# Adding the experts' results to rows in memory with accumulating scatters, and copying those rows to the output, in an attention and mixture-of-experts block

## The reference

```python
xn  = layernorm(x)
# attention: 16 heads of 8, causal
q, k, v = split(xn @ w_qkv)
a   = softmax(mask(q @ k.T / sqrt(8))) @ v @ w_proj + b_proj + xn
a   = layernorm(a) * gamma + beta
# experts: softmax over 8, the two best kept with their probabilities
y   = 0
for e in range(8):
    y += combine[:, e] * (gelu(xn @ W1[e] + b1[e]) @ W2[e] + b2[e])
out = x + a + y
```

## Time and profile before

| | |
|---|---|
| median of three runs | 837.65 us |
| the profiled execution | 838.32 us |
| its span, first to last instruction | 836.6 us |
| PE busy | 698.7 us (84%) |
| DVE busy | 653.4 us (78%) |
| POOL busy | 557.4 us (67%) |
| ACT busy | 544.8 us (65%) |
| moved by DMA | 93.66 MB, mean 112 GB/s |

### The profile page before, as it was taken

How to read it: one execution, slowest core, us unless ns; L and a number is a source line. 1 busy time by engine, 2 the same in 40 slices (tenths; PEclk the granted TensorE clock), 3 DMA queues, 4 the chain that set the end, 5 groups by cost and what they waited for, 6 DMA issues and landing times.

```text
span 836.6 us, 25028 instructions
## 1 busy us (share of the span) xinstructions
PE 698.7 (84%) x7876; PEld 518.2 (62%) x7878; DVE 653.4 (78%) x1550; ACT 544.8 (65%) x1107; POOL 557.4 (67%) x611
## 2 busy tenths in 40 slices
PE   2766989999999999999988878659999999999800
PEld 1543556666666666666656555338988889888700
DVE  5877978888978787878888887637878888888644
ACT  4812646666666666666756656538989999999700
POOL 8521758888877777777887786616766677667700
PEclk9987989999999999999999999869999999999955
DMA  9691323232322232223243333102222222222189
GB/s 271 230 312 59 94 68 100 89 102 89 101 90 100 91 100 91 99 92 107 84 148 120 111 107 93 28 14 73 87 83 80 86 87 82 86 77 90 49 277 333
DMA packets 113313, 93.66 MB, mean 112 GB/s; under 512 B 16618, under 2 KB 97650, under 8 KB 113268
## 3 DMA queue, kind: packets, MB, share of 16 engines
q1 hardware_dynamic: 95508, 70.26, 26.9%
q0 software_dynamic: 8704, 18.17, 6.1%
q10 hardware_dynamic: 9056, 4.66, 1.9%
HBM read 43.85 MB, written 48.93 MB: 111 GB/s over the span
## 4 chain that ended last, share of the span: by engine, by line
PE 60%; DVE 11%; ACT 7%; issue 7%; DMA 6%; POOL 6%; SPq 2%; ACTq 0%; POOLq 0%; DVEq 0%
PE wide L1323 11%; PE bank_head L1212 9%; PE bank_head L1314 5%; PE bank_maxB L1314 5%; PE wide L1177 5%; PE bank_maxA L1191 5%; DVE shift L966 4%; DMA xn_rows<-parts_dram 3%; PE bank_maxB L1191 3%; PE bank_maxA L1195 3%; PE wide L1181 3%; PE bank_misc L1237 3%; DMA pieces_f<-in_w 3%; POOL probs L601 2%; PE bank_maxB L1195 2%
## 5 line engine op out<-in xcount | busy, mean ns | idle before, releaser
L653 POOL DMA_INDIRECT parts_dram<-o_T,dest x144 | 161.3, 1120 | 75.9 <-issue 48.5
L601 POOL TENSOR_SCALAR_AFFINE_SELECT probs<-probs 128x512 f32<-128x512 f32 (+1 forms) x192 | 152.3, 805 | 83.1 <-ACT probs L687 81.0
L687 ACT ACTIVATE probs<-wide 128x1024 f32<-128x1024 f32 x192 | 185.4, 1023 | 31.1 <-PE wide L1177 18.9
L966 DVE TENSOR_REDUCE shift<-bank_maxA 128x2 f32<-128x512 f32 (+1 forms) x192 | 132.3, 689 | 52.4 <-PE bank_maxA L1195 48.7
L592 POOL DMA_INDIRECT x_slots<-xn_rows,slot_i x128 | 131.3, 1026 | 38.9 <-issue 37.5
L966 DVE TENSOR_REDUCE shift<-bank_maxB 128x2 f32<-128x512 f32 (+1 forms) x192 | 131.6, 685 | 5.4 <-PE bank_maxB L1195 1.3
L731 ACT ACTIVATE probs<-wide,b_all 128x256 f32<-128x256 f32 x288 | 121.5, 478 | 16.6 <-PE wide L1323 10.9
L1212 PE MATMUL bank_head<-probs,v_aug 128*32 128x256 f32 (+1 forms) x2048 | 99.6, 336 | 27.5 <-DVE x L992 22.9
L1323 PE MATMUL wide<-xgT_raw,xnT 128*128 128x256 f16 x864 | 109.3, 277 | 6.5 <-DVE xgT_raw L1073 6.5
L1212 PEld LDWEIGHTS bank_head<-probs,v_aug 128*32 128x32 f32 x2048 | 60.3, 112 | 72.3 <-issue 35.0
L1056 DVE TENSOR_TENSOR probs<-probs 128x512 f16<-128x512 f32 x144 | 99.7, 693 | 5.5 <-ACT probs L737 1.1
(11 more groups left out here) (178 smaller groups left out, 1253.3 us busy)
## 6 DMA issues: line engine op xcount, KB each, us to landing
qk_rows<-split SPq DMA_DIRECT2D x32, 512.0 KB, 3.0
x_slots<-fill SPq DMA_DIRECT2D x16, 598.5 KB, 7.8
fill<-x_slots SPq DMA_DIRECT2D x72, 133.0 KB
q_diag<-qk_rows SPq DMA_DIRECT2D x256, 32.0 KB, 1.8
k_cat<-qk_rows SPq DMA_DIRECT2D x64, 128.0 KB, 2.1
xn_rows<-parts_dram SPq DMA_DIRECT2D x8, 1024.0 KB, 11.7
x_all<-in_x SPq DMA_DIRECT2D x8, 512.0 KB, 7.5
pieces_f<-in_w SPq DMA_DIRECT2D x8, 512.0 KB, 4.0
```

The costliest lines, as they stand in the source:

```text
L601: pool.affine_select(out=part, in_=part, compare_op=ALU.is_ge, fill=0.0, base=0, pattern=[[0, n], [1, P]], channel_multiplier=-1).then_inc ...
L653: pool.indirect_dma_start(out=parts_dram, out_offset=bass.IndirectOffsetOnAxis(ap=dest[:, of, t:t + 1].bitcast(U32), axis=0), in_=y[:, of ...
L687: act.activation(probs[:, u, :], ps[:, :], ACT.Exp, scale=SCALE).then_inc(empty, 1)
L966: V.tensor_reduce(dst, ps[:, :].rearrange("p (j k) -> p j k", j=nh), axis=AX.X, op=ALU.max, negate=True).then_inc(empty, 1)
```

## The change

The rows that will be the output are now in memory from the start of the experts. `sum_rows` holds one row per token and the spare rows. During attention, SP stores each sequence's part of `x_all`, once the attention's result has been added to it (`begin_out(b)`, 32 stores of 128 KB). POOL's indirect DMAs then add their rows to `sum_rows` in memory (`compute_op=ALU.add`). A token has two picks with different experts, and two additions to one row must not be under way at once: so where the expert changes between two tiles, POOL waits until the three tiles before have landed. Whether it changes is worked out in registers from the packed list of experts: `whole` is 32 then, else 0, and with 0 the wait asks for nothing that is not there already. At the end, SP and ACT copy `sum_rows` to the output in four transfers from memory to memory, with no part in on-chip memory. The numbers behind a row lose one, so that a row of `xn_rows` has 132 elements and not 133.

```diff
-        parts_dram = nc.dram_tensor("parts_dram", [2 * B * T + NS * S, D], F32).ap()
+        sum_rows = nc.dram_tensor("sum_rows", [B * T + NS * S, D], F32).ap()
...
+            def begin_out(b):
+                sp.wait_ge(res_ready, b + 2)
+                sp.nop(nofuse=True)
+                sp.dma_start(sum_rows[bass.ds(b * T, T), :].rearrange("(t p) d -> p t d", p=P),
+                             x_all[:, bass.ds(b * QT, QT), :]).then_inc(out_begun, 16)
+            def stores(s):
+                return s - 2 - LAST >= 0 if isinstance(s, int) else True
...
+                if stores(s):
+                    begin_out(s - 2 - LAST)
...
             for u in range(2):
-                sp.wait_ge(sent[u], 32 * (NT // 2))
+                sp.wait_ge(sent[u], 32 * (NT // 2 - DEST_BUFS // 4))
+            for u in range(DEST_BUFS):
+                sp.wait_ge(placed[u], FIRST)
...
                 sp.dma_start(xg[:, quad, :, :], x_slots[bass.ds(s * S, S), :].rearrange("(t p) d -> p t d", p=P)).then_inc(xg_loaded[quad], 16)
+                if isinstance(s, int) and s in (1, 2):
+                    begin_out(B - 3 + s)
...
-            both = parts_dram[0:2 * B * T, :].rearrange("(t p c) d -> p t (c d)", p=P, c=2)
-            for c in range(LAST_CHUNKS):
-                if c >= PART_BUFS:
-                    sp.wait_ge(out_ready, c - PART_BUFS + 1)
-                sp.dma_start(parts[:, c % PART_BUFS, :, :], both[:, LC * c:LC * (c + 1), :]).then_inc(parts_loaded[c % PART_BUFS], 16)
+                sp.wait_ge(placed[u], 32 * (NS // DEST_BUFS) + FIRST)
+            for c in range(0, OUT_CHUNKS, 2):
+                rows = B * T // OUT_CHUNKS
+                sp.dma_start(out.rearrange("b (t p) d -> (b t) (p d)", p=16)[rows // 16 * c:rows // 16 * (c + 1), :],
+                             sum_rows[rows * c:rows * (c + 1), :].rearrange("(t p) d -> t (p d)", p=16)).then_inc(out_stored, 16)
+            sp.wait_ge(out_stored, 16 * OUT_CHUNKS)
...
+            pool.wait_ge(out_begun, 16 * B)
+            EVEN = sum((E - 1) << BITS * j for j in range(0, FIELDS - 1, 2))
+            ODD = sum((E - 1) << BITS * j for j in range(1, FIELDS - 1, 2))
+            def changes_at(i):
+                experts = experts_of(pool, i)
+                steps_up = (experts >> BITS) - (experts & (EVEN + ODD))
+                return (steps_up & EVEN) + EVEN, (steps_up & ODD) + ODD
+            def tile(s, k, changes):
+                if hides(s):
+                    u = s - 1
+                    of = (k - 1) % DEST_BUFS
+                    if beyond(u, 0):
+                        whole = changes[k % 2] >> (BITS * (k + 1) - 5) & 32 if BITS * (k + 1) > 5 else changes[k % 2] << (5 - BITS * (k + 1)) & 32
+                        for back in range(1, Y_BUFS):
+                            if beyond(u, back - 1):
+                                before = (k - 1 - back) % DEST_BUFS
+                                rounds = (s - k) * 4 - (0 if k >= 1 + back else 32)
+                                pool.wait_ge(placed[before], whole + (rounds + FIRST))
+                    pool.wait_ge(y_ready, u * 2 + 2)
                     pool.nop(nofuse=True)
                     for t in range(2):
-                        pool.indirect_dma_start(out=parts_dram, out_offset=bass.IndirectOffsetOnAxis(ap=dest[:, of, t:t + 1].bitcast(U32), axis=0),
-                                                in_=y[:, of % Y_BUFS, t, :], in_offset=None).then_inc(placed[of], 16)
-            tiles(pool, tile, load=False)
+                        pool.indirect_dma_start(out=sum_rows, out_offset=bass.IndirectOffsetOnAxis(ap=dest[:, of, t:t + 1].bitcast(U32), axis=0),
+                                                in_=y[:, of % Y_BUFS, t, :], in_offset=None,
+                                                compute_op=ALU.add).then_inc(placed[of], 16)
...
-            for c in range(LAST_CHUNKS):
-                act.wait_ge(out_ready, c + 1)
-                act.dma_start(out.rearrange("b (t p) d -> p (b t) d", p=P)[:, LC * c:LC * (c + 1), :],
-                              x_all[:, LC * c:LC * (c + 1), :]).then_inc(out_stored, 16)
-            act.wait_ge(out_stored, 16 * LAST_CHUNKS)
+            for u in range(DEST_BUFS):
+                act.wait_ge(placed[u], 32 * (NS // DEST_BUFS) + FIRST)
+            for c in range(1, OUT_CHUNKS, 2):
+                rows = B * T // OUT_CHUNKS
+                act.dma_start(out.rearrange("b (t p) d -> (b t) (p d)", p=16)[rows // 16 * c:rows // 16 * (c + 1), :],
+                             sum_rows[rows * c:rows * (c + 1), :].rearrange("(t p) d -> t (p d)", p=16)).then_inc(out_stored, 16)
...
-                dve.wait_ge(parts_loaded[c % PART_BUFS], 16 * (c // PART_BUFS + 1))
-                V.tensor_tensor(mine[:, :, 0:D], mine[:, :, 0:D], mine[:, :, D:2 * D], ALU.add).then_inc(parts_added, 1)
-                dve.wait_ge(parts_added, c + 1)
-                V.tensor_tensor(here, here, mine[:, :, 0:D], ALU.add).then_inc(out_ready, 1)
```

More of the change, by code:

```diff
@@ L238, in attention_and_moe @@
         placed = [sem(f"placed{u}") for u in range(DEST_BUFS)]
-        parts_loaded = [sem(f"parts_loaded{u}") for u in range(PART_BUFS)]
-        parts_added = sem("parts_added")
-        out_ready = sem("out_ready")
+        out_begun = sem("out_begun")
+        spare_ready = sem("spare_ready")
         out_stored = sem("out_stored")
@@ L312, in beyond, with steps @@
             return s > n if isinstance(s, int) else True
-        def steps(eng, step, after=((), ()), first_tile=None, written_out=False):
+        assert STAGES % 2 == 1
+        def steps(eng, step, after=((), ()), first_tile=None, written_out=False, in_loop=STAGES - 1):
             experts = None
-            first_whole = STAGES - 1 if not written_out else TAIL
+            first_whole = in_loop if not written_out else TAIL
             count = TAIL - first_whole
@@ L488, in _ @@
             load_experts()
-            sp.wait_ge(consts, 29)
-            steps(sp, step)
+            sp.wait_ge(consts, 27)
+            steps(sp, step, in_loop=STAGES + 1)
             for u in range(2):
-                sp.wait_ge(sent[u], 32 * (NT // 2))
+                sp.wait_ge(sent[u], 32 * (NT // 2 - DEST_BUFS // 4))
+            for u in range(DEST_BUFS):
+                sp.wait_ge(placed[u], FIRST)
             sp.wait_ge(packing, EXPERTS_PACKED)
@@ L659, in _ @@
+            changes = changes_at(0)
+            for s in range(UNROLL):
+                tile(s, s, changes)
+            with pool.Fori(0, NS // UNROLL - 1) as i:
+                changes = changes_at(i + 1)
+                for k in range(UNROLL):
+                    tile(i * UNROLL + (UNROLL + k), k, changes)
+            tile(NS, 0, changes_at(NS // UNROLL))
         @block.scalar
@@ L753, in tile @@
                     before = (k - 2 - Y_BUFS) % DEST_BUFS
-                    later(act, placed[before], (s - k) * 4 + (32 if k >= 2 + Y_BUFS else 0), beyond(s, 1 + Y_BUFS))
+                    later(act, placed[before], (s - k) * 4 + (32 + FIRST if k >= 2 + Y_BUFS else FIRST), beyond(s, 1 + Y_BUFS))
                     act.wait_ge(xg_used, s * 2 - 2)
@@ L919, in weights @@
                 then(V.tensor_reduce(red[:, :], prob[:, :, :], axis=AX.X, op=ALU.add))
-                V.tensor_scalar(xn_rows[:, :, D + 4], best[:, 0, :], -1.0, float(E), ALU.mult, ALU.add).then_inc(route, 1)
+                V.tensor_scalar(xn_rows[:, :, D + 3], best[:, 0, :], -1.0, float(E), ALU.mult, ALU.add).then_inc(route, 1)
                 route_count += 1
```

55 lines of the change are left out of this document (22 added, 33 removed).

## The result

The changed kernel takes 891.11 us (median of 4 runs, 885.89 to 893.77) beside 836.44 for the kernel before (4 runs, 835.06 to 838.79): a ratio of 1.064 [1.061, 1.067]. The forecast was 820 with a range up to 866. The profiled execution took 893.8 us (span 892.1), 55.5 more than the 838.3 against which the sum was made.

A forecast was written before the change was run, and what follows sets the result against it. PE was taken to set the expert tiles' pace and DMA transfers the end. From 838.3 us, -24.0 (end), +5.0 (first tile) and +1 (last scatter) gave 820, range 811 to 866.

The forecast's parts named there:

- The accumulating scatters: POOL's 144 scatters in the expert stage: adding in memory costs 0 us more each (bounds 0 and 0.96); last landing +1.
- POOL becomes the bound: Rival: longer descriptor lists slow POOL's scatters; at 0.4 us more each 866 us, by the skill page 877; chance 0.29.
- The 32 stores: SP's stores of x_all during attention fit into its idle 1.05 us per step: cost 0, without that cover 14 us.
- The first tile: Start of the experts: tile 0's load waits behind four stores, the last needing sequence 29's addition: +5.0 us, bounds 0 and 8.
- The end: After the last scatter: a 4 MB copy within memory replaces loads, additions and stores: -24.0 us, bounds -26.6 and -11.6.
- a slow copy: Rival at the end: memory is read and written at once, the copy takes 27 us, total 833 us; chance 0.11.
- POOL's registers: POOL's extra register operations per tile, some 0.3 us, lie under 2.3 us of scatters: cost 0.
- additions don't overlap: Rival in the scatters: each addition waits for its own read, 8 us per tile, over 1100 us; chance 0.05.

The follow-up runs named there:

- e1: The changed kernel with plain scatters in place of accumulating ones, waits, stores and copy kept: 824.97 us, 0.987 of the kernel before.
- e3: The changed kernel adding only to spare rows, without waits at expert changes, each added row half as long (64 elements): 875.14 us, 1.048 of the kernel before.
- e5: The kernel before plus 32 stores of x_all that nothing reads, at the change's places in SP's queue: 846.76 us, 1.012.
- e6: The kernel before plus the same 32 unread stores, moved behind the q and k store and the first four tile loads: 834.54 us, 0.998.

## Why the prediction was wrong

**The step that failed is *The accumulating scatters*.** It took 0 us more per scatter, out of bounds of 0 and 0.96; the runs show 0.58 by the medians (1544 to 960 in e1) and 0.48 by the means (1602 to 1120). Its reason, that scatters of 133 and 128 elements cost the same, was sound for what it compares (e3: rows of half the length cost the same, too), but it says nothing about another form of the instruction. I had called the step the weakest and read from the trace that 0.08 us was all it could bear; with that known, a cost that no row bounded better than 0.96 deserved more of the chance than 0.29. The rest of the sum can be read from e1_plain, where a scatter does cost nothing more: 824.97 beside 820. By the four lines of the table above its profile differs from the kernel before by +5.0, +4.8, 0 and -23.0, against 0, +5.0, 0 and -23.0 in the sum: what is left over lies in the steps, where the stores are.

In the stage of 290.4 us, the scatters' 230.6 - 161.3 = 69.3 less the 23.6 that the prediction found free makes +45.7. Of the remaining 62.6 - 45.7 = 16.9 us, 16.2 are the seven changes of expert, where the prediction put 11 and let the free time pay for them. The seven gaps are 2.54 to 2.76 us long, of which 0.30 is there anyway, so each wait cost 2.2 to 2.5 us where the prediction had up to 1.6. The waits were thus sized too small by a third, and they lost their cover once POOL was the bound. With plain scatters (e1) they cost nothing, as predicted.

**The rival *POOL becomes the bound* came true**, beyond the 866 that its 0.4 us gave. Its price from the Trainium skill's page "Collectives: The Full Stack", section "The bandwidth ceiling: the fold count and why AG ≠ RS ≠ AR", was 0.48 us more and 877: the size that was then measured. But by its mechanism, a price for each row, 64 rows should have cost half as much more, 0.24, and they cost 0.53. A packet for each added row is in the trace; POOL's time hardly follows it. The agreement was one of size only, and luck.

The Trainium skill's other page, "DMA: Bandwidth & Descriptors", section "Anatomy of one DMA — SWDGE (gpsimd) path", says that writing descriptors is a small part that grows noticeably only with many of them; the trace agrees as far as rows stand for descriptors, 1.0 to 1.8 ns a row here. The prediction took it as a second reason, beside its rows, to call the addition free, and that doesn't follow: the measurement decides, 0.53 to 0.58 us for the form.

***The 32 stores*** were put at 0, with 14 us if their cover was gone; 9.4 us more stand at the end of the steps in the change's profile (the first line of the table). The idle 1.05 us that I read in the earlier trace rows is from the looped steps, and there the shift is small: SP's store of q and k stands at 378.04 before and at 380.55 in the change, after three quarters of the sequences, and 0.8 of these 2.5 us were there ahead of the first store of `x_all`. From then on the gap widens to 9.4. In those steps SP loads a piece of the weights right behind the shifts, ACT waits for it, and the store went ahead of it. That a queue has room in one step is no proof for the steps that carry something more. That the place is the cause is shown by e5 and e6. The 9.4 itself is too much for it: in the seven profiled kernels with the stores at these places the last store of q and k stands at 503.7 to 510.4 (median 506.1), in the five others at 497.8 to 501.9 (median 501.1), so the place costs some 5 us there and the rest is the difference of two executions.

***The first tile*** was right in its mechanism and near in size: +5.0 predicted, +5.9 in the table. The timelines of POOL, SP and PE show the addition of sequence 29 ending at 555.13, the four stores held up behind it, and a wait of 5.49 us.

```profile
554.41 0.72 POOL L624 TENSOR_TENSOR x_all<-x_all,y 128x256 f32<-128x256 f32 x1 [1.80 <-ACT y L769]
```

```profile
541.18 14.40 SPq L455 DMA_DIRECT2D sum_rows<-x_all  x4
556.00 0.89 SPq L521 DMA_DIRECT2D fill<-x_slots  x2
```

```profile
558.60 0.69 PE L1335 MATMUL bank_maxA<-ident,fill 128*128 128x128 f32 x2 [5.49 <-DMA fill<-x_slots]
```

***The end*** was right: -24.0 predicted for a copy of 14.6 us; it took 15.8 (876.28 to 892.1) where the end had taken 38.6, so -22.8; the last scatter's landing took 0.4 us longer where +1 was put. The rival of a slow copy fell. ***POOL's registers*** show no cost: where POOL is the bound, the gap between two scatters is 0.30, the least there was before. The rival that additions don't overlap fell too: a whole scatter has landed a median of 3.3 us after its start, where 8 us per tile had been feared.

With the measured terms put in their places the sum is 838.3 + 9.4 + 5.9 + 45.7 + 16.9 - 22.4 = 893.8; this only lays the two profiles end to end and proves nothing more. The gain at the end was real and as large as forecast; nearly three times as much was then lost on POOL.

## What to carry to other kernels

Before work is moved from one engine into the descriptors of another, count how many such instructions the receiving engine issues and how much time each may grow before that engine is the bound (here 0.08 us); if no row shows the new form, give the bound's upper end its full chance. A scatter that adds in memory cost POOL over half as much again per instruction, with little difference between 64 and 128 rows and none between rows of 256 and 512 bytes, so it is worth trying where scatters are few or POOL has idle time; no run here shows a kernel in which it pays. A store that "fits" into a queue belongs behind the loads that somebody waits for, and the steps to check are those that carry an extra load, not the typical one.

## What the runs showed of the hardware

- An indirect DMA of 128 rows occupied POOL for 0.96 us plainly and for 1.54 us with an addition in memory; 64 rows took 0.90 and 1.43 us. With the addition, rows of 256 bytes took the same 1.54 us as rows of 512.
- An added row is a packet of its own (9,216 rows fewer, 9,216 packets fewer). POOL's queue took 14.4% of 16 engines over 892 us in the change and 6.1% of 823 us in e1_plain for the same bytes: (0.144 x 892.1 - 0.061 x 823.3) x 16 / 18,432 rows = 0.068 us of engine time more for each added row. That stayed hidden here.
- A copy of 4 MB within memory took 15.8 us, 4.0 us per megabyte with the landing, not far above the 3.2 of the mixed loads and stores before, although every byte is both read from memory and written to it.
- Loading 1 MB in 8 KB instead of 1 KB pieces landed in a median of 7.9 instead of 11.7 us with the engines full; the kernel as a whole gained 4.4 us (836.28 - 831.86).

What stays open is why the accumulating form costs POOL some 0.5 us more per instruction. A scatter of more than 128 rows, which might spread that price, was not tried. Nor does a run show what two additions to one row do when both are under way, against which the waits at the changes of expert stand.
